# A tower of embedding, convolution, attention and experts on one core: ten of 32 blocks of embedding rows by one-hot products on PE, and eight attention batches written out instead of looped

## The reference

```python
y = embed_table[x]                      # [8, 512, 256], table [500, 256]
h = depthwise_conv(y, 31 taps) + conv_b
q, k, v = split(layernorm(h) @ w_qkv)   # 16 heads of 64
q = softmax(q * SCALE, axis=-1); k = softmax(k, axis=-2)
context = einsum("bnd,bne->bde", q, k); out = einsum("bde,bnd->bne", context, v)
h = h + out @ w_out + b_out
# router: the 2 best of 8 experts for each token, 4 of width 256 and 4 of width 512
h = h + sum of the chosen experts' square(relu(xn @ w1)) @ w2, weighted
```

## Time and profile before

| | |
|---|---|
| median of 3 runs | 779.54 us (778.46 to 780.48) |
| the profiled execution | 778.08 us |
| its span, first to last instruction | 776.3 us |
| PE busy | 629.6 us, 81% of the span |
| POOL, DVE, ACT busy | 336.5, 470.6, 309.2 us |

### The profile page before, as it was taken

How to read it: one execution, slowest core, us unless ns; L and a number is a source line. 1 busy time by engine, 2 the same in 40 slices (tenths; PEclk the granted TensorE clock), 3 DMA queues, 4 the chain that set the end, 5 groups by cost and what they waited for, 6 DMA issues and landing times. The chain is left out here.

```text
span 776.3 us, 16107 instructions
## 1 busy us (share of the span) xinstructions
PE 629.6 (81%) x4950; PEld 545.7 (70%) x4950; DVE 470.6 (61%) x1218; ACT 309.2 (40%) x666; POOL 336.5 (43%) x312
## 2 busy tenths in 40 slices
PE   0179487999999999999999997307998998978873
PEld 0179366787777878878788775206997887878873
DVE  0157476687879778797887873636453454545441
ACT  3123025334453443535335354005553544455442
POOL 6733223230824608155271735142353443455474
PEclk9779789999999999999999999656998999999897
DMA  7470686010111102111020101332353444466563
GB/s 231 132 198 1 136 246 209 2 55 2 56 55 50 62 1 75 34 54 55 21 88 0 54 28 55 108 110 69 63 92 54 79 70 71 78 100 103 86 112 49
DMA packets 38621, 61.07 MB, mean 79 GB/s; under 512 B 6282, under 2 KB 31890, under 8 KB 37906
## 3 DMA queue, kind: packets, MB, share of 16 engines
q1 hardware_dynamic: 23266, 36.80, 16.2%
q0 software_dynamic: 14976, 22.10, 15.3%
q10 hardware_dynamic: 288, 1.05, 0.4%
HBM read 30.54 MB, written 28.34 MB: 76 GB/s over the span
## 5 line engine op out<-in xcount | busy, mean ns | idle before, releaser
L1440 POOL DMA_INDIRECT out<-y,token_at x72 | 113.1, 1571 | 128.9 <-SPq L1420 128.0
L701 POOL DMA_INDIRECT queue_d<-row,slot x64 | 64.1, 1002 | 164.0 <-DVE slot L1013 146.9
L1519 DVE SCALAR_TENSOR_TENSOR act_w<-relu,queue_rows 128x512 f32<-128x512 f32 (+1 forms) x72 | 45.6, 633 | 118.0 <-ACT relu L1464 97.7
L1177 PE MATMUL bank<-xt_hi,w_first 128*128 128x512 f32 x256 | 94.1, 413 | 0.9 <-DVE second_half L891 0.9
L1177 PE MATMUL bank<-w_first,xt_hi 128*128 128x512 f32 x256 | 84.0, 410 | 2.5 <-DVE xt_lo L881 1.5
L693 POOL TENSOR_TENSOR second_half<-second_half,q_inv 128x512 f32<-128x512 f32 x64 | 64.9, 1041 | 42.4 <-DVE q_inv L900 42.3
L751 ACT ACTIVATE second_half<-second_half 128x512 f32<-128x512 f32 x64 | 40.3, 631 | 88.0 <-DVE second_half L891 87.8
L759 ACT ACTIVATE k_exps<-bank,k_negmax 128x512 f32<-128x512 f32 x64 | 44.2, 691 | 75.1 <-DVE k_negmax L907 74.9
L1561 PE MATMUL bank<-w_hi,a_hi 128*128 x224 | 70.4, 314 | 0.4 <-DVE a_lo L1525 0.3
L1464 ACT ACTIVATE relu<-bank 128x512 f32<-128x512 f32 (+1 forms) x72 | 36.2, 503 | 77.3 <-PE bank L1561 77.3
L1561 PE MATMUL bank<-w_lo,a_hi 128*128 x224 | 63.8, 285 | 0.0
(11 more groups left out here) (174 smaller groups left out, 1570.6 us busy)
## 6 DMA issues: line engine op xcount, KB each, us to landing
queue_rows<-queue_d SPq DMA_DIRECT2D x74, 129.0 KB, 2.1
store<-in_L_ffn_w SPq DMA_DIRECT2D x4, 1536.0 KB, 9.2
out<-res SPq DMA_DIRECT2D x8, 512.0 KB, 2.9
h_d<-store SPq DMA_DIRECT2D x7, 512.0 KB, 8.9
h_in<-h_d SPq DMA_DIRECT2D x7, 512.0 KB, 3.9
wqk<-in_L_attn_w_qkv SPq DMA_DIRECT2D x1, 2048.0 KB, 8.0
queue_d<-filler SPq DMA_DIRECT2D x1, 1290.0 KB, 11.5
out<-y,token_at POOLq DMA_INDIRECT x72, 4.0
```

What stands on the lines that cost most here:

```text
L701: pool.indirect_dma_start(out=queue_d, in_=row[:, t, c, :], in_offset=None, out_offset=bass.IndirectOffsetOnAxis(ap=slot[:, TT * c + t:TT ...
L1177: last = nc.tensor.matmul(o, a, c, start=(n == 1), stop=(n == 3 * len(pairs)))
L1440: pool.indirect_dma_start(out=out, in_=y[:, j % RING, :], in_offset=None, compute_op=ALU.add, out_offset=bass.IndirectOffsetOnAxis(ap=toke ...
L1519: nc.vector.scalar_tensor_tensor(out=act_w[:, u % 2, 0:width], in0=relu[:, u % 2, 0:width], scalar=rows[:, u, DIM:DIM + 1], in1=relu[:, u ...
```

## The change

Three edits are made together.

1. POOL gathers 22 blocks of rows (`GATHERED`) instead of 32. The other ten (`PICKED`) are made on PE and DVE. ACT loads the whole table into `words` (four chunks of 128 words, the last padded with zeros by DVE). For each block, PE spreads the block's token numbers over all partitions (`spread`, one product with `ident`), DVE compares them with the word numbers (`take_hot`, 128x512), PE multiplies the four 128x128 one-hot matrices with the four chunks of the table (`pick`, four products of 128x256), and DVE copies the result into `rows` (`take_picked`, 128x256). All of it stands on PE and DVE ahead of the `wv` transposes and their copies. The waits for `gathered` count 22 blocks, and PE waits for all ten copies ahead of the `rw` transposes.
2. The engine loop of attend is gone: all steps are written out with constants, and there is no batch 8 (no load, norm, transposes, split or residual of it, and no store of batch 0 to `h_d`).
3. In experts, the branch of each turn after the first looks at the expert of tile 6 of the turn before instead of this turn's first tile.

```diff
+VOCAB = 500
+VC = -(-VOCAB // P)
+PICKED = 10
+GATHERED = BLK - PICKED
...
+    spare = store[:].rearrange("p a n -> p (a n)")
+    words = spare[:, 0:VC * DIM].rearrange("p (k c) -> p k c", k=VC)
+    hot = spare[:, VC * DIM:VC * DIM + 2 * VC * P].rearrange("p (n k t) -> p n k t", n=2, k=VC)
...
-            sp.wait_ge(gathered, 16 * BLK)
+            sp.wait_ge(gathered, 16 * GATHERED)
             sp.dma_start(wqk[:], w_qkv.rearrange("(k p) n -> p k n", p=P)[:, :, 0:2 * INNER]).then_inc(wqk_in, 16)
...
+            nc.gpsimd.iota(word_no[:], [[P, VC]], base=0, channel_multiplier=1,
+                           allow_small_or_imprecise_dtypes=True).then_inc(word_no_ready, 1)
             pool.wait_ge(ids_in, 16)
-            for i in range(BLK):
+            for i in range(GATHERED):
                 pool.indirect_dma_start(out=rows[:, BLK - 1 - i, :], out_offset=None, in_=embeddings,
...
         def _(act):
+            act.wait_ge(words_zero, 1)
+            whole = VOCAB // P
+            act.dma_start(words[:, 0:whole], embeddings[0:whole * P].rearrange("(k p) c -> p k c", p=P)
+                          ).then_inc(words_in, 16)
+            act.dma_start(words[0:VOCAB - whole * P, whole], embeddings[whole * P:VOCAB]).then_inc(words_in, 16)
             act.wait_ge(taps_out, 32)
...
         def _(dve):
+            nc.vector.memset(words[:, VC - 1], 0.0).then_inc(words_zero, 1)
             nc.vector.memset(padded[:], 0.0).then_inc(padded_zero, 1)
...
+            def take_hot(n):
+                dve.wait_ge(ids_spread, n + 1)
+                if n >= 2:
+                    dve.wait_ge(picked_psum, n - 1)
+                full = [P, VC, P]
+                nc.vector.tensor_tensor(hot[:, n % 2], bank[5 + n % 2][:, 0:P].unsqueeze(1).to_broadcast(full),
+                                        word_no[:].unsqueeze(2).to_broadcast(full), ALU.is_equal
+                                        ).then_inc(hot_ready, 1)
+
+            def take_picked(n):
+                dve.wait_ge(picked_psum, n + 1)
+                nc.vector.tensor_copy(rows[:, PICKED - 1 - n, :], bank[7 if n % 2 else 4][:, 0:DIM]
+                                      ).then_inc(picked, 1)
...
+            dve.wait_ge(ids_in, 16)
+            nc.vector.tensor_copy(ids_f[:], ids[:]).then_inc(ids_ready, 1)
+            dve.wait_ge(word_no_ready, 1)
+            take_hot(0)
+            for n in range(PICKED):
+                if n + 1 < PICKED:
+                    take_hot(n + 1)
+                take_picked(n)
             for n in range(4):
                 dve.wait_ge(wv_turned, n + 1)
...
+            def spread(n):
+
+                if n >= 2:
+                    pe.wait_ge(hot_ready, n - 1)
+                i = GATHERED + n
+                nc.tensor.matmul(bank[5 + n % 2][:, 0:P], ids_f[:, i:i + 1].to_broadcast([P, P]), ident[:],
+                                 start=True, stop=True).then_inc(ids_spread, 1)
+
+            def pick(n):
+                pe.wait_ge(hot_ready, n + 1)
+                if n >= 2:
+                    pe.wait_ge(picked, n - 1)
+                for k in range(VC):
+                    last = nc.tensor.matmul(bank[7 if n % 2 else 4][:, 0:DIM], hot[:, n % 2, k], words[:, k],
+                                            start=(k == 0), stop=(k == VC - 1))
+                last.then_inc(picked_psum, 1)
+
             pe.wait_ge(ident_ready, 1)
+            pe.wait_ge(ids_ready, 1)
+            spread(0)
+            spread(1)
+            pe.wait_ge(words_in, 32)
+            for n in range(PICKED):
+                pick(n)
+                if n + 2 < PICKED:
+                    spread(n + 2)
             pe.wait_ge(wv_in, 16)
...
             pe.wait_ge(rw_in, 16)
+            pe.wait_ge(picked, PICKED)
...
-            pe.wait_ge(gathered, 16 * BLK)
+            pe.wait_ge(gathered, 16 * GATHERED)
...
-        b = [Batch(n, n % 2, n // 2) for n in range(BATCHES)]
-        step(None, None, b[0], None)
-        step(b[0], None, b[1], None)
-        step(b[1], b[0], b[2], None)
-        with engine.Fori(1, BATCHES // 2) as i:
-            even, odd = Batch(i * 2, 0, i), Batch(i * 2 + 1, 1, i)
-            step(even, Batch(i * 2 - 1, 1, i - 1), odd, Batch(i * 2 - 2, 0, i - 1))
-
-            step(odd, even, Batch(i * 2 + 2, 0, i + 1), Batch(i * 2 - 1, 1, i - 1))
-        step(None, b[BATCHES - 1], None, b[BATCHES - 2])
-        step(None, None, None, b[BATCHES - 1])
+        batches = [Batch(n, n % 2, n // 2) for n in range(BATCHES)]
+
+        def at(n):
+            return batches[n] if 0 <= n < BATCHES else None
+
+        for n in range(-1, BATCHES + 2):
+            step(at(n), at(n - 1), at(n + 1), at(n - 2))
...
-                        for later in [*range(2, BATCHES), 0]:
+                        for later in range(2, BATCHES):
...
-            with engine.If((words[turn] & (EXPERTS - 1)) < WIDE):
+            first = words[turn] if turn == 0 else words[turn - 1] >> (3 * (SLOTS - AHEAD))
+
+            with engine.If((first & (EXPERTS - 1)) < WIDE):
```

More of the change, by code:

```diff
@@ L86, in is_first @@
     def is_first(self, count):
-        return isinstance(self.n, int) and self.n < count
+        return self.n < count
 class Dispatch:
@@ L217, in convolve @@
     wv = h_in[:].rearrange("p b t c -> p (b t c)").rearrange("p (k n) -> p k n", k=KC)
+    spare = store[:].rearrange("p a n -> p (a n)")
+    words = spare[:, 0:VC * DIM].rearrange("p (k c) -> p k c", k=VC)
+    hot = spare[:, VC * DIM:VC * DIM + 2 * VC * P].rearrange("p (n k t) -> p n k t", n=2, k=VC)
+    ids_f = sbuf("ids_f", [P, BLK])
+    word_no = sbuf("word_no", [P, VC])
+    words_zero, words_in, ids_ready, word_no_ready, ids_spread, hot_ready, picked_psum, picked = (sem(n) for n in (
+        "words_zero", "words_in", "ids_ready", "word_no_ready", "ids_spread", "hot_ready", "picked_psum", "picked"))
     ids_in, taps_in, bias_in, wqk_in, wv_in, wo_in = (sem(n) for n in (
@@ L586, in load @@
                 if b.is_first(3):
-                    sp.wait_ge(h_stored, 16 * (BATCHES - 1))
+                    sp.wait_ge(h_stored, 16 * (BATCHES - 2))
                     for par in range(2):
                         sp.wait_ge(loaded[par], 16)
-                first = b.n * SEQ if isinstance(b.n, int) else (b.n % BATCHES) * SEQ
-                sp.dma_start(h_in[:, b.par], h_d[bass.ds(first, SEQ), :].rearrange("(p t) c -> p t c", t=TT)
+                sp.dma_start(h_in[:, b.par], h_d[b.n * SEQ:b.n * SEQ + SEQ, :].rearrange("(p t) c -> p t c", t=TT)
                              ).then_inc(loaded[b.par], 16)
@@ L607, in store_h2 @@
                 sp.wait_ge(res_added, b.nth(2, 2))
-                sp.dma_start(out[bass.ds(b.n * SEQ, SEQ), :].rearrange("(p t) c -> p t c", t=TT), res[:, b.par]
+                sp.dma_start(out[b.n * SEQ:b.n * SEQ + SEQ, :].rearrange("(p t) c -> p t c", t=TT), res[:, b.par]
                              ).then_inc(stored[b.par], 16)
```

## The result

The changed kernel took 774.19 us in the median of 16 executions (768.23 to 780.62), the kernel before 779.62 (775.57 to 782.66), so the ratio is 0.9926 with a 95% interval from 0.9901 to 0.9951. The ratios here are formed from fast executions alone and need not be the quotient of the medians. That is faster, by 0.7% or some 6 us and not by the 15.5 forecast, and outside the range of 758 to 772. The profiled execution took 768.23 us, the shortest of the 16. The same kernel was measured twice more later, and there it was slower than the kernel before: 788.11 us against 778.82 (ratio 1.0125, 1.0066 to 1.0184) and 790.58 against 779.86 (1.0129, 1.0095 to 1.0162).

A forecast was written before the change was run, and what follows sets the result against it. PE was taken to bound steady attention, with a large idle engine only in the first stage. Gains of 12.5 + 1.2 + 0.84 + 1.0 = 15.5 us off 778.08 gave 762.5, plus 1.46 a median of 764.0; range 758 to 772.

The forecast's parts named there:

- The gather, the picks, the clock: First stage: ten gathers fewer, rows at 32.0, 12.5 us won; convolution starting at full clock, 1.2 us won.
- Attention written out, batch 8 gone: Attention: no back edges or loop entry, 0.84 us won; last step without batch 8's work, 1.0 us won.
- The branch of the experts: Experts: same code runs, total of pauses between turns taken as unchanged, 5 us on either side as bound.
- the back edge's 0.4 us: Attention loop: back-edge row of 0.4 us, taken to decide against 6 us from two back edges at 3 us each.
- The median stands 1.46 above that execution.: Whole kernel: the median's distance from the profiled execution, added to 762.5 to give 764.0 us.
- PE is ready 2 us before the rows are, and the work costs nothing as long as that cover lasts: First stage: PE free at 29.9, rows at 32.0; cover gone if pick with spread costs 2.15 us, not 1.95.
- the rival that PE or DVE comes later than the rows: First stage: picks outlast the gathers; likely size 2 to 8 us, about 769 us; chance 0.17.
- the port that POOL and DVE share: First stage: DVE's PSUM operations taken to hold up no gather; other bound 11.1 us, rows at 43.1.

The follow-up runs named there:

- e3: The kernel before with only the experts' branch changed to look at tile 6 of the turn before; 781.95 us, ratio 1.0039.
- e6: The changed kernel with the old branch condition, written with one shift more; 789.70 us, ratio 1.0129.
- e2: The kernel before with only attention written out and batch 8 gone; 787.98 us, ratio 1.0113.
- e9: The changed kernel itself, measured a third time; 790.58 us, ratio 1.0129.
- e13: The kernel before, run once more for a second profile; 780.32 us in one execution.
- e10: The changed kernel with POOL's first gather issued only after the tenth pick; 800.98 us, ratio 1.0260.
- e14: The changed kernel with at most one gather under way; 819.51 us, ratio 1.0462.
- e15: The changed kernel with at most two gathers under way, two semaphores in turn; 786.79 us, ratio 1.0079.
- e17: The kernel before with the picks edit, gathers 3 to 9 with two under way at most, the rest at POOL's pace; 798.75 us, ratio 1.0246.
- e18: As e17, with 24 small transposes more on PE ahead of its wait for the gathers; 774.86 us, ratio 0.9956.
- e1: The kernel before with only the picks edit, attention loop and experts' branch as before; 804.29 us, ratio 1.0317.
- e7: The changed kernel with 32 small products added at the end of PE's list in attend; 789.50 us, ratio 1.0108.
- e8: The changed kernel with 64 small products added at the end of PE's list in attend; 787.01 us, ratio 1.0123.
- e4: The changed kernel with the experts' branch condition of the kernel before; 788.25 us, ratio 1.0115.
- e11: The changed kernel with the loads of windows, wv, rw and biases issued after the tenth pick; 800.47 us, ratio 1.0253.
- e12: The changed kernel with ACT instead of DVE copying the ten picked blocks from PSUM; 787.95 us, ratio 1.0092.
- e16: The changed kernel with all ten spreads and compares first, then all products, one increment per pair; 784.44 us, ratio 1.0031.

## Why the prediction was wrong

In the first measurement the steps can be read one by one. Of the 10.2 us between the forecast of 764.0 and the median, 5.7 lie in the profiled execution (768.23 for 762.5) and 4.5 in the distance of the median from it.

- **The gather, the picks, the clock.** Right. Rows at 32.23 for 32.0; picks over at 28.2 for 27.3, with 3.75 us for the first one, twice the 1.89 of the later ones, as at the half clock; 1.95 us each after that; PE idle 2.05 for 2.1; compare 0.68, copy 0.42; a granted clock of 1.00 at the convolution. `xt` of batch 0 comes at 81.38 for 94.73: 13.35 us against 13.7 forecast.
- **Attention written out, batch 8 gone.** Right in kind. From that `xt` to PE's first queued row it takes 428.17 us for 431.15, 3.0 us against 1.84.
- **The branch of the experts: "I take the same total".** This is the step that failed. From the first queued row to the end it takes 256.8 us for 250.5, with 9.7 us more in the chain's pauses. I had kept 5 us on either side. The kernel before has six pauses of 1 us and more, from 2.60 (and not 3.0) to 4.65 us, the changed kernel nine, up to 7.39. The three add up: 13.35 + 2.98 - 6.35 = 9.98, the difference of the spans, 776.3 - 766.4. The cause is not edit 3, as e3 and e6 show, but edit 2: e2 has 33.3 us of pauses, and so it is in all 14 traces with written-out attention. I had weighed the fetch of code only inside attention and read the back edge's 0.4 us as proof that it is cheap. The 0.4 us hold for the place that the loop's code has in the kernel before.
- **"The median stands 1.46 above that execution."** For the changed kernel it stands 5.96 above. No trace of one of the longer executions of that measurement exists. Shorter standstills among the picks would fit; that was not shown.

In the later measurements the step "PE is ready 2 us before the rows are, and the work costs nothing as long as that cover lasts" fails too. I named the rival that PE or DVE comes later than the rows and sized it at 2 to 8 us; in e9 the rows are there at 32 and the first `turn` is at 49.45, 17 us later. I had looked for it in durations and in the port that POOL and DVE share. It was neither: the durations on DVE and the gathers' 1.25 us are as forecast, and PE is held up. (After a standstill PE also falls back to the half clock: e9's pick at 20.14 takes 3.68 us.) Against e13's profile, e9's `xt` of batch 0 comes 3.0 us later (98.80 for 95.77), attention takes 1.65 us less, the experts 8.8 us more (259.8 for 251.0): 10.1 us, the difference of the spans.

The wait that the new work put between PE and DVE is the reason that it matters. The kernel before has the same late words (e13), under 18 us of slack.

**Two causes, and how far they are shown.** That the standstill needs several gathers under way is shown both ways: none beside the picks, or one or two at a time, and it is gone in all five traces (e10, e14, e15, and e17 and e18, which hold back the first nine); the other loads taken away, and it stays, as in all ten later traces with picks beside unpaced gathers, on three chips. They are not enough by themselves, since the first profile has the same gathers and no standstill; by what way they hold PE up is not shown. That the place of PE's code decides over the back edges is shown by e17 and e18, with the fetched blocks beside it. Counting weight loads, products and the other recorded instructions of PE, the first back edge is its 3,409th instruction in the kernel before, the 3,617th in e1 and e17 (208 later) and the 3,667th in e18 (258 later; about 256 was aimed at). The Trainium skill (Runtime: NRT & Kernel Launch, Instruction fetch mechanics) gives PE room for 2,048 instructions, filled in blocks of 256, and says that a taken branch out of the fetched window stalls for a fetch. The loop's body has some 1,640 instructions here, which touches seven or eight such blocks according to where it starts. The runs agree with blocks of that size, since 16 KB come with each packet and a shift by about one block brings back the short back edge, and with the stall after a taken branch in e1 and e17. Where the blocks begin no trace shows, so that the number of blocks touched is what decides is an argument, not a finding. The same section speaks for unrolling. Written-out attention, with batch 8 gone, takes 3 us less here, but the measurement decides against it: 33 us of pauses for 24.

**What stays open.** Why written-out attention lengthens the pauses between turns: the packets in the pauses point to the fetch of code, but shifts of 64 and 128 instructions (e7, e8) did not undo it, and others were not tried. And why the first measurement had no long standstill; its chip is not on record. One thing differs in the traces: of the updates of the gathers' semaphore, 16 for each gather, the first two traces hold 512 of 512 (before) and 351 of 352 (after), those of e1, e4 to e9, e11, e12 and e16 hold 59 to 98 of 352, and of 512 e2 holds 161, e3 121 and e13 164; e14 holds all 352 and e15 317; between them are e10 with 217, e17 with 150 and e18 with 145, whose gathers pile up only after the picks or late among them. Where gathers piled up after the first measurement, PE or its words were late and records are missing; in the first measurement they piled up as well, and neither is seen. Every execution here was recorded, so no run tells whether the recording takes a part in the standstill. The Trainium skill (NOTIFIC — Programmer's Manual, The design, and what it trades) says that a full queue of records can be set to overwrite the oldest, to drop new ones or to stall the one that writes; no run here shows which is the case.

## What to carry to other kernels

Before work is moved into an idle stretch of an engine, see in the profile not only how long the engine is idle but how promptly its words arrive there: a hand-over per step next to a stream of indirect DMAs waited here for the last of them, and a limit of two under way kept it prompt. Any edit that changes the length of PE's list ahead of a loop moves the loop against the blocks of code; count the instruction queue's packets before and after, and try a shift before the edit is judged. And measure the changed kernel again beside each group of variants: without that, edit 3 would have passed for worth 14 us.

## What the runs showed that was not expected

- 48 short instructions on an idle PE made the kernel 24 us faster (798.75 to 774.86), with 66 and 47 packets of code; 18 of the 66 fall in two passes of a loop that fetches nothing in the other place.
- A back edge of a loop cost 0.4 us in one place and 7.9 to 11.3 us in another, and the granted clock of the step fell from 1.00 to as low as 0.91.
- While indirect DMAs pile up, PE passes one product in some 2 us (e16), and its increments reach DVE up to 18 us after the product's recorded end (e9) and ACT up to 16 us (e12); DVE's increments reach PE at once (in e9 the compare from 19.39 to 20.08 is followed by the pick at 20.14).
- e18, with ten picks, the loop, paced gathers and a shifted list, is the only version here that beat the kernel before outside the first measurement, by 0.44%.
